# Moving the last addition of a softmax sum from VectorE to GpSimd, one weight-building unit behind the first output projection, and one weight load later

## The chip, the cores and the metric

The kernel runs on one NeuronCore of a Trainium2 chip. The metric is the device time of one execution in microseconds. The profile of one execution gives a span (first to last instruction) and, for every instruction, its start and its duration. Engines are written as in the profile: PE (TensorE), DVE (VectorE), ACT (ScalarE), POOL (GpSimd), SP (SyncE, which here only issues DMAs).

## The reference, cut to what matters

A graph of 512 nodes with 512 features goes through four residual layers: an attention layer with a feed-forward part, two GIN convolutions, a GCN layer and two relational (RGCN) layers. The change touches the attention and one weight of the relational layers.

```python
q, k, v = ((x @ W + b).reshape(N, H, HEAD) for W, b in ((Wq, bq), (Wk, bk), (Wv, bv)))
scores = jnp.einsum('nhd,mhd->nhm', q, k) / np.sqrt(HEAD)
scores = jnp.where(adj[:, None, :] == 0, -1000000000.0, scores)
attn = jax.nn.softmax(scores, axis=1)          # over the 8 heads, not over the nodes
attn_out = jnp.einsum('nhm,mhd->nhd', attn, v).reshape(N, D_OUT) @ Wo + bo
h1 = _layer_norm(x + attn_out, g1, be1)
...
w = jnp.einsum('rb,bio->rio', att, basis)      # relational weights from 30 bases
agg + x @ root + bias
```

## The kernel before

**The softmax over the heads.** The 512 x 512 scores of 8 heads are made in eight steps, `it` = 0 to 7. A step holds 128 nodes m on the partitions, 256 nodes n and the 8 heads, 128 x 2048 numbers. Since the softmax runs over the heads, its maximum and its sum are elementwise trees over the eight head slices: 4 + 4, 2 + 2, 1 + 1.

**One step, engine by engine.** PE writes the scores of step it+1 to the PSUM tensor `sbank` (`products`, L1490, and `exclude`, L1498, which masks missing edges), then the weighted sum of step it-1 (`attend`, L1513), then some units (below). ACT copies half of the scores (L616), DVE finds the maximum (`find_max`, L962 to L964) and subtracts it (`centre`, L1038, two instructions), ACT takes exp in place (L600). DVE then sums the heads in three additions: L1049 (128x1024 out), L1050 (128x512) and L1053 (128x256, into `row_sum`). ACT makes the reciprocal as exp(-ln) (`invert`, L608 and L610, each behind the loading of an activation table). Four heads are multiplied by it on DVE (L1065), four on POOL (`scale_heads`, L426); in the last step DVE multiplies all eight. The order of DVE's queue in one step is: L1049, L1050, L1053 of step it; L962, L963, L964 and the two of L1038 for step it+1; L1065 of step it; in steps 0 and 1 also the addition of a bias to a tile of v (L875).

**Where a product may start.** `products(it+1, pair)` overwrites the half of `sbank` that `centre(it)` has read. `attend(it)` waits for both multiplications of step it. `project(0)`, the first of four output projections (L1567), needs the first half of `centre(7)`, since it writes over that part of `sbank`.

**Units.** The relational weights are sums over 30 bases with 32 units per layer (64 in all). A unit is a DMA of 1 MB into a ring of four places (`bring`; L336 on SP's queue, issued when the unit four places earlier has been used) and eight matmuls of PE (L1357). They are put between other work by hand; `STEP_UNITS` is how many follow each attention step. Each fourth unit ACT copies the sums to `stage` and SP stores them.

**After the last step.** PE's order is `project(0)`, `attend(6)`, `project(1)`, `attend(7)`, one unit, `project(2)`, `project(3)`. `project(2)` waits for ACT's `take_ao(1)` (L621), which takes the result of `attend(7)` out of PSUM. On ACT's queue `take_ao(1)` stands behind `root(1, 0)` and `root(1, 1)`, the square roots (L466) of the norm of the first two projected tiles. DVE makes that norm tile by tile: L1082 (residual), L853 and L858 (statistics), L1073, L863, L1075; L1082 of tile 0 stands in DVE's queue behind L1065 of step 7.

**Weights.** POOL's queue issues the weight loads (`load_weight`, L398), each when the last reader of the place it overwrites is done (`LAST_READ`). `root1` is a weight of 1 MB for the first relational layer. It is loaded when `c2_1` is done ("c2_1_psum"). ACT and DVE split it into two parts after the GCN aggregation (`split_weight("root1")`, L490 and L1015). Between `c2_1` and that, PE has the transposes L1668 ("x4_psum"), units 55 to 59, and the aggregation over k (L1411) in the parts k = 0, unit 60, k = 1 to 3, unit 61; part k waits for `h_gcn_lo(k)` of DVE (L1208).

Of the kernel before, what the change touches and what calls it, by code (L numbers as in the profile page):

```python
# [25 lines left out]
ALU = mybir.AluOpType  # L26
# [5 lines left out]
C = D // P  # L32
# [52 lines left out]
def in_extra(n):  # L85

    return any(n in pair for pair in EXTRAS)


RING_UNITS = [n for n in range(2 * UNITS) if not in_extra(n)]  # L90
STEP_UNITS = (1, 2, 3, 3, 3, 3, 3, 0)
ATTENTION_BATCHES = (EARLY_UNITS + sum(STEP_UNITS)) // BATCH + 1
AGG0_BATCHES = 11

# [15 lines left out]
             "f2b": ("weight_parts", 2 * C), "c1_0": ("ff1_psum", C), "lin": ("ff1_psum", 2 * C),  # L110
             "c2_0": ("ff2_psum", C), "c1_1": ("ff2_psum", C),
             "c2_1": ("weight_parts", 7 * C), "gcn": ("weight_parts", 8 * C),
             "root1": ("c2_1_psum", C), "root2": ("c2_1_psum", C)}

AGG2_BANKS = H1T_BANKS = (0, 1, 4, 5)
T_ORDER = ("h1T", "ff1", "ff1_second", "hT2", "agg0", "agg1", "agg2")
# [12 lines left out]
def build(nc, x, src, dst, etype, weights, rows, cols, alphas, att, basis, scratch, out):  # L129
    with ExitStack() as ctx:  # L130
# [5 lines left out]
        def sem(name):  # L136
            if name not in names:
                names[name] = ctx.enter_context(nc.semaphore(name))
            return names[name]
# [5 lines left out]
        def places(*uses):  # L145

            made = []
            for use in uses[:-1]:
                with ExitStack() as early:
                    made += [early.enter_context(nc.sbuf_tensor(*t)) for t in use]  # L150
            return made + [ctx.enter_context(nc.sbuf_tensor(*t)) for t in uses[-1]]
# [10 lines left out]
        no_edge, row_sum, sum_tmp, adj, adjT_r = places(  # L162
            [("no_edge", [P, C, N], BF16), ("row_sum", [P, 2, N // 2], F32), ("sum_tmp", [P, 2, N // 2], F32)],
            [("adj", [P, C, N], F32)], [("adjT_r", [P, C, N], F32R)])
# [68 lines left out]
        four_sums = adjT[:, 0:2, :].rearrange("p c (a n) -> p (c a) n", a=2)  # L233
# [8 lines left out]
        def row(name):  # L242
            return rring[:, ROWS.index(name) % RSLOTS, :]
# [59 lines left out]
        def probs_of(it):  # L303
            return s01[:, (it % 2) * C:(it % 2 + 1) * C, :].rearrange("p c (a n) -> p (c a) n", a=2)
# [8 lines left out]
        def blk(t, c):  # L313
            return slice(c * t, (c + 1) * t)

        with nc.Block() as block:
# [54 lines left out]
            def _(pool):  # L371
# [22 lines left out]
                def load_weight(name):  # L394
                    i = WEIGHTS.index(name)
                    last, tiles = LAST_READ[name]
                    pool.wait_ge(sem(last), tiles)
                    pool.dma_start(weight(name), weights[i]).then_inc(sem(f"weight_{PLACE[name]}_loaded"), 16)  # L398

                def load_row(name, last):  # L400
                    i = ROWS.index(name)
                    pool.wait_ge(sem(last), C)
                    pool.dma_start(row(name), rows[i, :].partition_broadcast(P)).then_inc(
                        sem(f"row_slot{i % RSLOTS}_loaded"), 16)
# [18 lines left out]
                def scale_heads(it):  # L423
                    sc = probs_of(it)
                    pool.wait_ge(sem("row_inverse"), 2 * it + 2)
                    pool.tensor_tensor(sc[:, OWN_HEADS:, :], sc[:, OWN_HEADS:, :],  # L426
                                       row_sum[:, 1:2, :].to_broadcast([P, HEADS - OWN_HEADS, N // 2]),
                                       ALU.mult).then_inc(sem("pool_probs"), 1)

                scale_heads(0)  # L430
                scale_heads(1)
                load_row("g2", "v")
                for it in range(2, 2 * C - 1):
                    scale_heads(it)
                pool.wait_ge(sem("pv_used"), 2 * C)
                load_weight("f1b")
                pool.wait_ge(sem("o_psum"), C)
# [24 lines left out]
            def _(act):  # L462
# [133 lines left out]
                def exps(it):  # L596
                    for half in range(2):
                        act.wait_ge(sem("centred"), 2 * it + half + 1)
                        sc = probs_of(it)[:, 4 * half:4 * half + 4, :]
                        act.activation(sc, sc, ACT.Exp).then_inc(sem("exped"), 1)  # L600
# [25 lines left out]
                for it in range(2 * C):  # L626
# [5 lines left out]
                    if it + 1 < 2 * C:  # L632
                        exps(it + 1)
                    stage_units(STEP_UNITS[it])
                    if C - 1 <= it < 2 * C - 1:
# [180 lines left out]
            def _(dve):  # L816
                steps = [0]

                def step(ins):

                    steps[0] += 1
                    ins.then_inc(sem("dve_step"), 1)
                    return steps[0]

                def after(n):
                    dve.wait_ge(sem("dve_step"), n)
# [218 lines left out]
                for it in range(2 * C):  # L1045
                    sc = probs_of(it)
                    dve.wait_ge(sem("centred"), 2 * it + 2)
                    dve.wait_ge(sem("exped"), 2 * it + 2)
                    after(step(dve.tensor_tensor(four_sums, sc[:, 0:4, :], sc[:, 4:8, :], ALU.add)))  # L1049
                    after(step(dve.tensor_tensor(sum_tmp[:, :, :], four_sums[:, 0:2, :], four_sums[:, 2:4, :], ALU.add)))  # L1050
                    if it:
                        dve.wait_ge(sem("probs"), it)
                    dve.tensor_tensor(row_sum[:, 0, :], sum_tmp[:, 0, :], sum_tmp[:, 1, :], ALU.add).then_inc(  # L1053
                        sem("row_sum"), 1)
                    if it + 1 < 2 * C:
                        dve.wait_ge(sem("scores_psum"), 4 * it + 8)
                        dve.wait_ge(sem("scores"), it + 2)
                        find_max()
                        centre(it + 1)
                    if it == 2 * C - 1:  # L1060
                        split_weight("f1a")
                    dve.wait_ge(sem("row_inverse"), 2 * it + 2)
                    heads = OWN_HEADS if it < 2 * C - 1 else HEADS
                    own = sc[:, 0:heads, :]
                    dve.tensor_tensor(own, own, row_sum[:, 1:2, :].to_broadcast([P, heads, NH]),  # L1065
                                      ALU.mult).then_inc(sem("probs"), 1)
                    if it < 2:
                        take_v(2 + it)
# [259 lines left out]
            def _(pe):  # L1328
# [13 lines left out]
                def units(n):  # L1342


                    for u in (next(unit) for _ in range(n)):
                        b, g = divmod(u, BATCH)
                        if u == 0:
                            pe.wait_ge(sem("att_ready"), BATCH)
                        if g == 0 and b >= 2:
                            pe.wait_ge(sem("stage_ready"), b - 1)  # L1350
                        if g == 0 and b == EARLY_UNITS // BATCH:
                            pe.wait_ge(sem("v"), 1)
                        elif g == 0 and b == EARLY_UNITS // BATCH + 1:
                            pe.wait_ge(sem("v"), C)
                        wait_unit(pe, u)
                        for j in range(COLT):
                            mm = pe.matmul(unit_bank(b)[32 * j:32 * j + 32, :], attw[0:KB, u // UNITS, g, :],  # L1357
                                           unit_place(u)[0:KB, j, :], start=(g == 0), stop=(g == BATCH - 1),
                                           tile_position=(0, 32 * j), skip_group_check=True)
                        mm.then_inc(sem("basis_used"), 1)  # L1360
# [198 lines left out]
                def project(c):  # L1559

                    pe.wait_ge(sem("ao"), 2 if c < 2 else 4)
                    if c == 0:
                        need_weight(pe, "o")
                    if c < 2:
                        pe.wait_ge(sem("centred"), 4 * C - 1)
                    for k in range(C):
                        mm = pe.matmul(bank[C + c][:, :], qT[:, k, blk(P, c)], weight("o")[:, k, :], start=(k == 0),  # L1567
                                       stop=(k == C - 1))
                    mm.then_inc(sem("o_psum"), 1)

                pe.wait_ge(sem("no_edge"), C)
                for it in range(2 * C):
                    if it + 1 < 2 * C:
                        for pair in range(2):
                            products(it + 1, pair)
                            exclude(it + 1, pair, "scores_psum")
                    if it == 2 * C - 1:
                        project(0)
                    if it:
                        attend(it - 1)  # L1580
                    if it == 2 * C - 1:
                        project(1)
                    if it < 2:
                        qkv_tile(2 * C + 2 + it)
                    units(STEP_UNITS[it])
                attend(2 * C - 1)
                units(1)
                project(2)
# [218 lines left out]
```

## Time and profile before

| | |
|---|---|
| three runs | 455.17, 455.60, 456.53 us, median 455.6 |
| the profiled execution, its own time | 459.73 us |
| its span | 457.9 us, 1.8 us less than its own time |
| busy share of the span | PE 96%, DVE 76%, ACT 53%, POOL 9% |
| mean granted clock of TensorE | 0.993 |
| DMA | 99.22 MB, mean 217 GB/s |

The profiled execution is one execution, and it was longer than each of the three timed ones. The attention steps lie between 88 and 165 us of its span. Times in the rows are microseconds from the start of the span.

### The profile page before, as it was taken

What the parts mean: (1) busy time and instruction counts of PE and PEld (TensorE: products, weight loads), DVE (VectorE), ACT (ScalarE), POOL (GpSimd) and SP (SyncE); (2) the same over time, 40 slices, a digit from 0 to 9 for tenths busy, and PEclk for the clock granted to TensorE, in tenths of its full rate; (3) what the DMA queues carried; (4) which work ended last, traced back from release to release, by engine and by line L of the source; (5) the groups of instructions that cost most, each with busy time, mean ns of one, the idle gap of its engine ahead of it and who ended that gap; (6) DMA issues with size and microseconds to landing.
All of it is one profiled execution on the core that took longest, in us unless ns stands there. A gap on an engine that the chain in (4) does not pass through costs nothing.

```text
span 457.9 us, 6200 instructions
## 1 busy us (share of the span) xinstructions
PE 441.6 (96%) x2226; PEld 275.4 (60%) x2226; DVE 346.4 (76%) x736; ACT 243.6 (53%) x428; POOL 42.7 (9%) x59
## 2 busy tenths in 40 slices
PE   8999999899997999999999999999989999999997
PEld 3334453444432345768756867677357688888885
DVE  5999996899999849785879675766778695866212
ACT  5999994676897516562246335535662523511210
POOL 3240000024224002000010000010000000000000
PEclk9999999999999799999999999999999999999999
DMA  7997348426699747979089856687871740000002
GB/s 258 414 392 170 115 167 324 160 92 233 245 374 353 278 192 250 424 263 383 36 336 342 318 213 285 247 320 284 318 250 49 290 178 16 1 0 2 0 3 92
DMA packets 18090, 99.22 MB, mean 217 GB/s; under 512 B 2959, under 2 KB 3599, under 8 KB 7567
## 3 DMA queue, kind: packets, MB, share of 16 engines
q1 hardware_dynamic: 13191, 72.72, 42.4%
q0 software_dynamic: 4000, 25.18, 14.9%
q10 hardware_dynamic: 864, 0.86, 0.6%
q8 instruction: 22, 0.36, 0.3%
q14 instruction: 13, 0.11, 0.1%
HBM read 93.50 MB, written 5.25 MB: 216 GB/s over the span
## 4 chain that ended last, share of the span: by engine, by line
PE 72%; DVE 14%; DMA 10%; issue 2%; ACT 1%; DVEq 0%; SPq 0%
PE bank L1371 20%; PE sbank L1703 10%; DMA bring<-in_basis 7%; PE bank L1716 6%; PE sbank L1357 6%; PE sbank L1427 6%; PE sbank L1567 4%; PE bank L1688 4%; PE bank L1450 3%; PE bank L1357 3%; PE bank L1411 2%; DVE stat L853 2%; PE sbank L1411 2%; DMA wring<-in_weights 2%; PE bank L1513 2%; PE sbank L1490 2%
## 5 line engine op out<-in xcount | busy, mean ns | idle before, releaser
L1357 PE MATMUL sbank<-bring,attw 120*32 120x512 f32 x336 | 41.0, 599 | 2.2 <-DMA bring<-in_basis 2.2
L839 DVE TENSOR_SCALAR cnt<-iota_row,edge_f 128x512 bf16<-128x512 f16 x132 | 41.2, 347 | 0.4 <-PE sbank L1427 0.4
L466 ACT ACTIVATE stat<-stat,eps 128x1 f32<-128x1 f32 x32 | 9.4, 294 | 42.9 <-DVE stat L858 42.9
L1427 PE MATMUL sbank<-cnt,adjT 128*128 128x512 bf16 x132 | 30.6, 380 | 0.3
L576 ACT ACTIVATE adjT<-distance,edge_w,edge_f 128x128 bf16<-128x128 bf16 x61 | 29.3, 480 | 1.4 <-PE sbank L1427 1.4
L1281 DVE SCALAR_TENSOR_TENSOR y_lo<-sbank,gate,y_hi 128x512 fp32r<-128x512 f32 x16 | 11.8, 750 | 22.6 <-ACT y_hi L765 22.5
L497 ACT ACTIVATE s<-bank,colsb 128x512 f32<-128x512 f32 x24 | 16.4, 687 | 21.8 <-PE bank L1371 21.8
L1427 PEld LDWEIGHTS sbank<-cnt,adjT 128*128 128x128 bf16 x132 | 12.3, 98 | 21.7 <-DVE cnt L839 6.4
L1371 PE MATMUL bank<-hT_hi,w_hi 128*128 128x512 f32 x64 | 25.3, 395 | 0.0
L529 ACT ACTIVATE distance<-iota_row,edge_f 128x128 bf16<-128x128 f16 x61 | 24.3, 400 | 1.8 <-DVE edge_f L905 0.4
L1371 PE MATMUL bank<-hT_hi,w_lo 128*128 128x512 f32 x64 | 24.9, 390 | 0.0
L1371 PE MATMUL bank<-hT_lo,w_hi 128*128 128x512 f32 x64 | 24.9, 389 | 0.0
L1703 PE MATMUL sbank<-w_hi,xT_hi 128*128 128x512 f32 x64 | 24.9, 389 | 0.0
L1703 PE MATMUL sbank<-w_lo,xT_hi 128*128 128x512 f32 x64 | 24.9, 389 | 0.0
L1703 PE MATMUL sbank<-w_hi,xT_lo 128*128 128x512 f32 x64 | 24.9, 389 | 0.0
L836 DVE TENSOR_SCALAR adjT<-iota_row,edge_f,edge_w 128x128 bf16<-128x128 f16 x71 | 22.1, 312 | 2.0 <-PE sbank L1427 2.0
L765 ACT ACTIVATE y_hi<-sbank,gate 128x512 fp32r<-128x512 f32 x16 | 10.8, 688 | 23.8 <-PE sbank L1703 23.8
L1357 PE MATMUL bank<-bring,attw 120*32 120x512 f32 x144 | 19.0, 627 | 4.0 <-DMA bring<-in_basis 4.0
L600 ACT ACTIVATE s<-s 128x1024 f32<-128x1024 f32 x16 | 16.9, 1058 | 11.1 <-DVE s L1038 10.6
L426 POOL TENSOR_TENSOR s<-s,row_sum 128x1024 f32<-128x1024 f32 x7 | 16.6, 2374 | 59.1 <-ACT row_sum L610 59.1
L1357 PEld LDWEIGHTS sbank<-bring,attw 120*32 120x32 f32 x336 | 8.5, 109 | 22.0 <-issue 20.2
L1490 PE MATMUL sbank<-qkw 64*128 64x256 f32 x128 | 18.1, 402 | 2.1 <-DVE s L1038 2.0
(250 smaller groups left out, 1095.9 us busy)
## 6 DMA issues: line engine op xcount, KB each, us to landing
bring<-in_basis SPq DMA_DIRECT2D x59, 1024.0 KB, 9.7
wring<-in_weights POOLq DMA_DIRECT2D x8, 1024.0 KB, 10.0
landing<-in_weights POOLq DMA_DIRECT2D x4, 1024.0 KB, 5.1
w_scratch<-stage SPq DMA_DIRECT2D x16, 256.0 KB
hT<-in_weights POOLq DMA_DIRECT2D x4, 1024.0 KB, 8.4
qkw<-w_scratch POOLq DMA_DIRECT2D x2, 2048.0 KB, 8.0
rring<-in_rows POOLq DMA_DIRECT2D x12, 256.0 KB, 8.3
wring<-in_basis SPq DMA_DIRECT2D x2, 1024.0 KB, 12.9
```

The lines of the kernel that those rows point to most:

```text
L529: act.activation(distance[:, i % 2, :], iota[:, 0:P], ACT.Abs, scale=-1.0, bias=dst_lo[:, n:n + 1]).then_inc(sem("distance"), 1)
L576: act.activation(hot_d[:, n % HOT, :], distance[:, i % 2, :], ACT.Relu, scale=minus_w[:, n:n + 1], bias=weight_f[:, n:n + 1]).then_inc(sem ...
L836: dve.tensor_scalar(hot_d[:, n % HOT, :], iota[:, 0:P], dst_lo[:, n:n + 1], weight_f[:, n:n + 1], ALU.is_equal, ALU.mult).then_inc(sem("ho ...
L839: dve.tensor_scalar(hot_s[:, n % HOT, :], iota[:, :], src_f[:, n:n + 1], None, ALU.is_equal).then_inc(sem("hot_ready"), 1)
L1357: mm = pe.matmul(unit_bank(b)[32 * j:32 * j + 32, :], attw[0:KB, u // UNITS, g, :], unit_place(u)[0:KB, j, :], start=(g == 0), stop=(g == ...
L1371: mm = pe.matmul(bank[c][:, :], lhs[:, k, blk(P, c)], rhs[:, k, :], start=(k == 0 and i == j), stop=(k == C - 1 and i == 1))
L1411: mm = pe.matmul(bank[banks[c]][:, :], x[:, k, blk(P, c)].bitcast(dt), counts[:, k, :], start=(k == 0 and i == 0), stop=(k == C - 1 and i ...
L1427: pe.matmul(bank[7][:, :], hot_d[:, n % HOT, :], hot_s[:, n % HOT, :], start=(n == 0), stop=(n == ECH - 1)).then_inc(sem("hot_used"), 1)
L1490: pe.matmul(sbank[:, place_of(h), :], kT[at:at + HD, h // 2, blk(P, m)], qT[at:at + HD, h // 2, blk(NH, half_n)], start=(a == 0), stop=Fal ...
L1567: mm = pe.matmul(bank[C + c][:, :], qT[:, k, blk(P, c)], weight("o")[:, k, :], start=(k == 0), stop=(k == C - 1))
L1703: mm = pe.matmul(bank[C + c][:, :], (xT_hi, xT_lo)[i][:, k, blk(P, c)], (w_hi, w_lo)[j][:, rel * C + k, :], start=(k == 0 and i == j), sto ...
L1716: mm = pe.matmul(bank[c][:, :], counts[:, k, blk(P, c)], y[:, k, :].bitcast(dt), start=False, stop=(rel == RELS - 1 and k == C - 1 and i = ...
```

## The change

Of each step's three additions the last one goes from DVE to POOL: DVE signals `pair_sums` behind L1050, POOL adds the two halves into `row_sum`, and ACT waits for POOL's signal as it did for DVE's. POOL's queue then alternates: addition of step it, multiplication of step it (steps 0 to 6), and the addition of step 7. One unit goes from step 5 and is put behind `project(0)` in step 7; the number of units up to `attend(7)` stays 18. `root1` is loaded when the transposes L1668 are done, no longer when `c2_1` is.

```diff
-STEP_UNITS = (1, 2, 3, 3, 3, 3, 3, 0)
+STEP_UNITS = (1, 2, 3, 3, 3, 2, 3, 1)
...
-             "root1": ("c2_1_psum", C), "root2": ("c2_1_psum", C)}
+             "root1": ("x4_psum", C), "root2": ("c2_1_psum", C)}
...
-                scale_heads(0)
-                scale_heads(1)
-                load_row("g2", "v")
-                for it in range(2, 2 * C - 1):
+                def add_pairs(it):
+
+                    pool.wait_ge(sem("pair_sums"), it + 1)
+                    if it:
+                        pool.wait_ge(sem("row_inverse"), 2 * it)
+                    pool.tensor_tensor(row_sum[:, 0, :], sum_tmp[:, 0, :], sum_tmp[:, 1, :], ALU.add).then_inc(
+                        sem("row_sum"), 1)
+
+                for it in range(2 * C - 1):
+                    add_pairs(it)
                     scale_heads(it)
+                    if it == 1:
+                        load_row("g2", "v")
+                add_pairs(2 * C - 1)
...
-                    after(step(dve.tensor_tensor(sum_tmp[:, :, :], four_sums[:, 0:2, :], four_sums[:, 2:4, :], ALU.add)))
                     if it:
-                        dve.wait_ge(sem("probs"), it)
-                    dve.tensor_tensor(row_sum[:, 0, :], sum_tmp[:, 0, :], sum_tmp[:, 1, :], ALU.add).then_inc(
-                        sem("row_sum"), 1)
+                        dve.wait_ge(sem("row_sum"), it)
+                    dve.tensor_tensor(sum_tmp[:, :, :], four_sums[:, 0:2, :], four_sums[:, 2:4, :], ALU.add).then_inc(
+                        sem("pair_sums"), 1)
...
                     if it == 2 * C - 1:
                         project(0)
+                        units(STEP_UNITS[it])
                     if it:
                         attend(it - 1)
                     if it == 2 * C - 1:
                         project(1)
                     if it < 2:
                         qkv_tile(2 * C + 2 + it)
-                    units(STEP_UNITS[it])
+                    if it < 2 * C - 1:
+                        units(STEP_UNITS[it])
```

## Rows read from the trace of the kernel before

**Rows 1.** Stretches of the span: length, busy time of each engine, PEclk, DMA share, GB/s.

```profile
127.00:149.40 22.40, 17.97 (x140) 6.60 (x134) 21.95 (x24) 19.82 (x25) 7.11 (x3) 0.99 0.96 364
149.40:151.30 1.90, 1.90 (x9) 0.24 (x9) 1.86 (x3) 1.88 (x3) 0.00 (x0) 0.50 0.92 328
```

**Rows 2.** Timeline of PE, steps 5 to 7: start, duration, engine, line, idle before.

```profile
138.80 1.06 PE L1357 MATMUL bank<-bring,attw 120*32 120x512 f32 x8 [1.50 <-DMA bring<-in_basis]
...
146.98 1.06 PE L1357 MATMUL bank<-bring,attw 120*32 120x512 f32 x8 [1.03 <-DMA bring<-in_basis]
149.36 1.94 PE L1357 MATMUL bank<-bring,attw 120*32 120x512 f32 x8 [1.31 <-DMA bring<-in_basis]
151.22 5.97 PE L1567 MATMUL sbank<-wring,qkw 128*128 128x512 f32 x8
...
159.00 3.70 PE L1567 MATMUL sbank<-wring,qkw 128*128 128x512 f32 x8
...
165.75 7.13 PE L1567 MATMUL sbank<-wring,qkw 128*128 128x512 f32 x16 [0.18 <-ACT qkw L621]
```

**Rows 3.** Timeline of DVE: step 0, the end of step 2, and step 6 onward.

```profile
89.33 1.23 DVE L1049 TENSOR_TENSOR adjT<-s 128x1024 f32<-128x1024 f32 x1
...
91.31 0.43 DVE L1053 TENSOR_TENSOR row_sum<-sum_tmp 128x256 f32<-128x256 f32 x1
...
113.96 1.70 DVE L1065 TENSOR_TENSOR s<-s,row_sum 128x1024 f32<-128x1024 f32 x1
115.58 1.21 DVE L1049 TENSOR_TENSOR adjT<-s 128x1024 f32<-128x1024 f32 x1
...
145.65 2.36 DVE L1038 TENSOR_TENSOR s<-sbank,softmax_tmp 128x1024 f32<-128x1024 f32 x2
...
149.43 1.21 DVE L1049 TENSOR_TENSOR adjT<-s 128x1024 f32<-128x1024 f32 x1
...
154.15 2.28 DVE L1065 TENSOR_TENSOR s<-s,row_sum 128x2048 f32<-128x2048 f32 x1
157.43 0.69 DVE L1082 TENSOR_TENSOR vr<-sbank,hr 128x512 f32<-128x512 f32 x1 [0.99 <-PE sbank L1567]
...
159.96 0.75 DVE L1075 SCALAR_TENSOR_TENSOR vr<-vr,stat,rring 128x512 f32<-128x512 f32 x1
162.74 0.69 DVE L1082 TENSOR_TENSOR vr<-sbank,hr 128x512 f32<-128x512 f32 x1 [2.03 <-PE sbank L1567]
```

**Rows 4.** Groups of DVE by line, 86 to 160 us: count, busy us, mean ns.

```profile
L875 DVE TENSOR_TENSOR vr<-bank,rring 128x512 f32<-128x512 f32 x4 | 2.6, 680 | 0.0
```

**Rows 5.** Timeline of ACT, step 0: the reciprocal.

```profile
91.77 0.42 ACT L608 ACTIVATE row_sum<-row_sum 128x256 f32<-128x256 f32 x1 [0.35 <-DVE row_sum L1053]
...
93.50 0.42 ACT L610 ACTIVATE row_sum<-row_sum 128x256 f32<-128x256 f32 x1
```

**Rows 6.** Timeline of POOL: the multiplications of steps 0 and 2.

```profile
94.00 2.38 POOL L426 TENSOR_TENSOR s<-s,row_sum 128x1024 f32<-128x1024 f32 x1 [24.02 <-ACT row_sum L610]
...
112.20 2.37 POOL L426 TENSOR_TENSOR s<-s,row_sum 128x1024 f32<-128x1024 f32 x1 [4.38 <-ACT row_sum L610]
```

**Rows 7.** Groups of POOL by line, whole span: another computing instruction.

```profile
L388 POOL COPY attw<-attw 120x16 f32<-120x16 f32 x3 | 1.6, 557 | 14.6 <-DMA attw<-in_att 14.6
```

**Rows 8.** Timelines of POOL, PE and DVE around the load of `root1`.

```profile
321.06 0.53 POOL L398 DMA_DIRECT2D wring<-in_weights  x1 [18.93 <-PE bank L1371]
...
329.49 1.07 PE L1357 MATMUL sbank<-bring,attw 120*32 120x512 f32 x8 [0.90 <-DMA bring<-in_basis]
...
334.63 1.06 PE L1357 MATMUL sbank<-bring,attw 120*32 120x512 f32 x8 [1.29 <-DMA bring<-in_basis]
...
337.40 0.69 DVE L1208 TENSOR_TENSOR root_lo<-hr,root_hi 128x512 fp32r<-128x512 f32 x1 [1.54 <-ACT root_hi L738]
...
339.38 0.39 PE L1411 MATMUL bank<-adjT_r,root_hi 128*128 128x512 f32 x1
...
341.96 2.20 ACT L490 CAST root_hi<-wring 128x512 fp32r<-128x512 f32 x4
```

## The prediction

> **What bounds the kernel now.** I read the page's slices first (PE busy nearly everywhere, its clock low in one slice), then the chain that ended last, then the timelines of each engine between 88 and 166 us and the stretches cut out of them. The chain names DMA and PE for the end of the attention: from step 5 on PE stands before units whose data have not landed, 1.50, 1.03 and 1.31 us in the three longest waits, while the DMA engines are 96% busy [rows 1, 2]. Behind the last wait the granted clock is 0.50, the 1.2 GHz level; a unit takes 1.94 us in place of 1.06, `project(0)` 5.97 in place of the 3.70 of `project(1)` [rows 1, 2]. That half clock cost 0.88 + 2.27 = 3.15 us.
>
> The reader must see a second chain beside it. DVE has 21.95 us of work in the 22.40 us from 127 on [rows 1], and in most steps it doesn't run at its own speed. Its L1065 takes 1.70 us while POOL is still multiplying; POOL ends at 112.20 + 2.37 = 114.57, L1065 at 115.66, and the next step's L1049 starts at 115.58, 1.01 behind POOL's end [rows 3, 6]. The same 1.00 or 1.01 stands behind POOL's end in steps 4, 5 and 6. So a step of DVE is a loop of latency: sums, reciprocal on ACT, POOL's multiplication, 1.01 us, next step.
>
> How the two chains meet decides what a gain is worth. DVE's L1065 of step 7 ends at 154.15 + 2.28 = 156.43. Behind it stand the norm of tile 0, 159.96 + 0.75 - 157.43 = 3.28 (3.20 to the next start, which overlaps), and from tile 1's L1082 through `root(1, 1)` and `take_ao(1)` to `project(2)` 165.75 - 162.74 = 3.01 [rows 2, 3]. Starting 0.08 before L1065's end, as the next instruction does at 115.58, that is 156.43 - 0.08 + 3.20 + 3.01 = 162.56. PE alone would have been there at 165.75 - 0.18 = 165.57, or at 162.42 had its clock stayed up [rows 2]. In an execution with a full clock the DVE chain and the PE chain arrive together, and taking waits off PE alone buys nothing.
>
> Which kind are the timed executions? The profiled one took 459.73 us, the median of the runs is 455.6, which is 4.1 less, and 3.15 of these are the price of the half clock. I take the timed runs as mostly free of it, with a chance of 0.7. My sum is made for the profiled execution and then read against the median.
>
> **The change part by part.**
>
> *The unit.* Step 5 loses the unit that waited 1.50, and the last of step 6's becomes the one behind `project(0)`. The first half of `centre(7)` is over near 145.65 + 1.2 = 146.9 [rows 3], so `project(0)` can start about 147 in place of 151.22, and the DMA gets the 3.7 us of `project(0)` to bring the last unit. The load of the fourth unit after that of step 5 is issued later too, which leaves more of the busy DMA to the two before it. PE's own path gets 4 us shorter (7 with the clock). The cover for what is late next is gone with it: PE is early and waits for DVE.
>
> *The addition.* DVE loses eight L1053 of 0.43 [rows 3]. They would pay only if DVE's queue were the loop. What the loop sees is the way from L1050's end to ACT's logarithm: now 0.04 + 0.43 + 0.03, from 91.27 to 91.77 [rows 3, 5]. Then it is a handover to POOL, the addition, and a handover to ACT. Handover: ACT's end at 93.92 to POOL's start at 94.00 is 0.08 [rows 5, 6]; DVE to ACT is 0.04. The price of a 128x256 addition on POOL isn't in the trace. From below: a quarter of 2.37, 0.59 [rows 6]. From above: all of the 557 ns of the small copy as a fixed cost plus a quarter of the rest, 0.56 + 1.81 / 4 = 1.01 [rows 7]. The row nearest in kind is the multiplication, the copy has a strided pattern, so both ends are unlikely; I take the middle, 0.80. The way becomes 0.08 + 0.80 + 0.04 = 0.92, that is 0.42 more than 0.50.
>
> The Trainium skill, GPSIMD Engine Reference, section 3.1, gives 4497 ns for a float32 `tensor_tensor` addition of 2048 elements; with the row of 1024 elements a straight line gives an estimate of 0.78, and the sum below would be 0.2 us smaller by it. Its section 1 speaks against this change: POOL shares its SBUF interfaces with VectorE and contends with instructions that have two SBUF inputs. L1065 is one, and the 1.70 beside 1.21 for the same size without POOL agrees; L962 has a PSUM input and should not feel POOL's addition.
>
> Now the loop. In step 0 POOL's multiplication ends 96.38 - 89.33 = 7.05 behind L1049's start [rows 3, 6]; that becomes 7.47, and with 1.01 behind it a step takes 8.48. DVE's earlier `centre` can't help, since L1065 then only waits longer beside POOL. Steps 0 and 1 have a v tile besides, 0.60 each to the next start (0.68 with the overlap) [rows 4]. Seven steps: 7 x 8.48 + 1.20 = 60.56, so step 7 starts at 89.33 + 60.56 = 149.89, now 149.43 [rows 3]: 0.46 later. Step 7: L1049 and L1050 take 1.94, the way 0.92, the reciprocal from 91.77 to 93.92 takes 2.15 [rows 5], a handover 0.07: L1065 starts at 154.97 and ends at 157.25, 0.82 later than 156.43. `project(2)` then starts at 162.56 + 0.82 = 163.38. Against the profiled 165.75 that is 2.37 earlier, against an execution with a full clock 0.82 later. With 0.59 for the addition, each of eight ways is 0.21 shorter: 1.7 less; with 1.01, 1.7 more. POOL's remaining queue hides nothing of worth: the issue of `g2` stands behind the multiplication of step 1 and in front of the addition of step 2, and waits for a v tile that DVE makes before that step's sums, 2 us ahead.
>
> *The root weight.* Its load is now issued at 321.06, just when the ring's loads for units 59 and 60 are [rows 8]. Both units wait, 0.90 and 1.29. Issued when the transposes are done, some 4 us later (near 325), it leaves the first unit the bus alone; 1 MB at the 364 GB/s of a busy stretch [rows 1] is some 2.9 us. Of the 2.19 not all is gain: the aggregation's last part starts at 339.38, and needs the L1208 that ends at 337.40 + 0.69 = 338.09 and hangs on no unit [rows 8]. With 0.05 for the handover it can start at most 1.2 earlier; DVE's split of the next weight behind it holds nothing more. I take 1.1. The weight itself is read at 341.96 [rows 8], about 17 us after its new issue. Bounds: 0, if unit 60 is still late beside it, and 1.2.
>
> *Sum.* For an execution like the profiled one 459.73 - 2.37 - 1.1 = 456.3, with a full clock behind the change. Against the median: 455.6 + 0.82 - 1.1 = 455.3.
>
> **The rivals.**
>
> *The waits and the half clock are in the timed runs too (chance 0.24).* For it: the only execution with a trace has them. Against it: 4.1 us between it and the median. Then 455.6 - 2.37 - 1.1 = 452.1, faster.
>
> *The clock falls in a new gap (0.20), the case on the other side.* PE ends `attend(7)` near 159.2 (157.3, when L1065 is done, + 1.9) and the unit near 160.2, and then stands until 163.4: a gap of 3.2 us where a full-clock execution before has almost none. In the rows a gap of 1.50 left the clock up, gaps of 1.03 and 1.31 with one unit between brought it down [rows 1, 2]. If it falls, `project(2)` pays what `project(0)` paid, about 2.3: 455.3 + 2.3 = 457.6, slower. It decides once the gap is above some 2.3 us. The Trainium skill, TensorE: Matmul & The Clock Gate, Part 1, says that the array falls to half rate when it has been idle and regains the full one after sustained work; the trace agrees at 149.4. By that rule the longer gap makes this rival stronger than the one before it.
>
> *GpSimd's addition is dear (0.07)*: at 1.01 us and in every step on the loop, 455.3 + 1.7 = 457.0.
>
> *It is cheap (0.09)*: at 0.59, and the DVE chain gains: 455.3 - 1.7 = 453.6. A variant of it is that DVE's own queue is the loop after all and its 0.43 per step count.
>
> **How the numbers follow.** My case, the two parts nearly cancelling, has 0.40. I call 0.3% (1.4 us) what a measurement can tell from no change. My case is the same with 0.34, faster with 0.05, slower with 0.01; the first rival faster with 0.24; the clock rival slower with 0.20; the dear addition slower with 0.05 and the same with 0.02; the cheap one faster with 0.07 and the same with 0.02. That makes 0.36 faster, 0.38 the same, 0.26 slower. The range reaches to the first two rivals, 452.0 to 457.8. My case alone, by half of the spread of the addition and the bounds of `root1`: 454.3 to 456.6.
>
> **What would show it.** POOL has eight additions of about 0.8 us, each starting 0.08 behind L1050's end. L1049 starts 8.4 to 8.5 us apart, and L1065 takes 1.7 to 1.9 in every step, nowhere 1.21. No unit waits more than 0.5 us in step 6; `project(0)` starts at 147 and takes 3.7; PE's wait has moved to before `project(2)`, released by ACT's L621, at 163.4, and L1065 of step 7 ends near 157.3. Units 59 and 60 wait less than 0.5 us together. I am wrong if L1065 of step 7 ends before 156.4 (the loop isn't POOL's), if the clock is 0.50 anywhere behind 160, or if the runs gain 3 us, which would say that the timed executions before had the half clock.

## The result

The changed kernel takes 459.95 us in the median of four runs (459.44 to 460.67), the kernel before 456.06 in the median of four (455.17 to 456.70). The ratio is 1.0087, 95% interval 1.0067 to 1.0108: slower by 3.9 us, outside the range of the prediction and past its rival on the other side (457.6).

Every run lists its mean granted clock of TensorE, and that is the first thing to read here. In the four runs of the changed kernel it was 0.992 or 0.993. Of the kernel before, 34 runs beside the first experiments have a clock each (a 35th took 888 us and isn't counted): 22 of them 0.999 or 1.000, with a median of 456.12 us, 12 of them 0.949 to 0.996, with a median of 457.53. The profiled execution of before (0.993) was one of the rarer kind.

### The profile page after: what moved, and what is told of

Same layout as the page of the kernel before. It is cut to its first block, busy times and chain, and to the rows that moved or that the text cites. A ratio compares the mean times of both kernels' runs of the same rounds, so it can differ in the third digit from the quotient of the medians.

```text
span 458.2 us, 6207 instructions
## 1 busy us (share of the span) xinstructions
PE 441.5 (96%) x2226; PEld 276.9 (60%) x2226; DVE 346.7 (76%) x728; ACT 243.3 (53%) x428; POOL 49.4 (11%) x67
## 4 chain that ended last, share of the span: by engine, by line
PE 70%; DVE 18%; issue 4%; DMA 4%; ACT 2%; POOL 1%; DVEq 0%; SPq 0%; POOLq 0%
PE bank L1379 22%; PE sbank L1713 9%; PE sbank L1365 7%; PE bank L1726 6%; PE sbank L1435 6%; PE bank L1618 5%; PE bank L1698 4%; DVE s L1047 3%; DMA bring<-in_basis 3%; PE bank L1419 3%; PE sbank L1419 2%; PE bank L1458 2%; PE sbank L1345 2%; PE sbank L1575 2%; DVE softmax_tmp L971 2%
## 5 line engine op out<-in xcount | busy, mean ns | idle before, releaser
L1365 PE MATMUL sbank<-bring,attw 120*32 120x512 f32 x336 | 41.0, 599 | 3.1 <-DMA bring<-in_basis 3.1
L1365 PEld LDWEIGHTS sbank<-bring,attw 120*32 120x32 f32 x336 | 8.6, 109 | 22.6 <-issue 22.6
L1498 PE MATMUL sbank<-qkw 64*128 64x256 f32 x128 | 18.2, 402 | 3.2 <-DVE s L1047 3.0
L1047 DVE TENSOR_TENSOR s<-sbank,softmax_tmp 128x1024 f32<-128x1024 f32 x16 | 18.8, 1219 | 1.1 <-DVE softmax_tmp L973 0.8
L1498 PEld LDWEIGHTS sbank<-qkw 64*128 64x128 f32 x128 | 11.1, 186 | 13.8 <-DVE s L1047 7.4
```

The costliest lines, as they stand in the source:

```text
L1047: dve.tensor_tensor(sc[:, heads, :], sbank[:, heads, :], tmp[:, 0:1, :].to_broadcast([P, 4, NH]), ALU.subtract).then_inc(sem("centred"), 1)
L1498: pe.matmul(sbank[:, place_of(h), :], kT[at:at + HD, h // 2, blk(P, m)], qT[at:at + HD, h // 2, blk(NH, half_n)], start=(a == 0), stop=Fal ...
```

## The profile after

Timeline of PE in the changed kernel, steps 5 to 7 and behind (L1498 are the products, L1365 the units, L1575 the projections).

```profile
134.89 1.92 PE L1365 MATMUL bank<-bring,attw 120*32 120x512 f32 x16
138.19 1.13 PE L1498 MATMUL sbank<-qkw 64*128 64x256 f32 x8 [1.37 <-DVE s L1047]
...
146.37 1.07 PE L1365 MATMUL bank<-bring,attw 120*32 120x512 f32 x8 [1.17 <-DMA bring<-in_basis]
147.36 3.70 PE L1575 MATMUL sbank<-wring,qkw 128*128 128x512 f32 x8
151.00 1.06 PE L1365 MATMUL bank<-bring,attw 120*32 120x512 f32 x8
...
159.38 1.07 PE L1365 MATMUL bank<-bring,attw 120*32 120x512 f32 x8
163.10 8.83 PE L1575 MATMUL sbank<-wring,qkw 128*128 128x512 f32 x16 [2.65 <-ACT qkw L630]
```

It answers to [rows 2]. Three waits for DMA have become one (the wait of 1.37 is for VectorE), `project(0)` starts at 147.36 in place of 151.22 and runs at full clock. Then PE stands 2.65 us before `project(2)`, and the two projections behind it take 8.83 us where they took 7.13. The stretches show why (length, busy time of PE, PEld, DVE, ACT, POOL, clock, DMA share, GB/s):

```profile
160.00:162.00 2.00, 0.44 (x7) 0.00 (x0) 1.90 (x5) 0.21 (x2) 0.33 (x1) 1.00 0.51 160
162.00:164.00 2.00, 0.90 (x2) 0.49 (x3) 1.37 (x3) 1.04 (x3) 0.00 (x0) 0.98 0.99 418
164.00:166.00 2.00, 2.00 (x4) 0.78 (x3) 0.00 (x0) 0.00 (x0) 0.00 (x0) 0.50 1.03 434
166.00:168.00 2.00, 2.00 (x5) 0.85 (x4) 0.00 (x0) 0.00 (x0) 0.00 (x0) 0.67 0.32 135
```

The half clock has moved from before `project(0)` [rows 1] to behind the gap. DVE, to be read against [rows 3]:

```profile
89.50 1.22 DVE L1058 TENSOR_TENSOR adjT<-s 128x1024 f32<-128x1024 f32 x1
...
115.87 1.21 DVE L1058 TENSOR_TENSOR adjT<-s 128x1024 f32<-128x1024 f32 x1
...
122.44 1.88 DVE L1073 TENSOR_TENSOR s<-s,row_sum 128x1024 f32<-128x1024 f32 x1
124.24 1.21 DVE L1058 TENSOR_TENSOR adjT<-s 128x1024 f32<-128x1024 f32 x1
...
149.39 1.21 DVE L1058 TENSOR_TENSOR adjT<-s 128x1024 f32<-128x1024 f32 x1
150.63 0.69 DVE L1061 TENSOR_TENSOR sum_tmp<-adjT 128x512 f32<-128x512 f32 x1
151.24 3.02 DVE L1024 TENSOR_TENSOR w_lo<-landing,w_hi 128x512 fp32r<-128x512 f32 x4
154.72 2.29 DVE L1073 TENSOR_TENSOR s<-s,row_sum 128x2048 f32<-128x2048 f32 x1 [0.46 <-ACT row_sum L619]
```

POOL, to be read against [rows 6]:

```profile
117.89 0.73 POOL L435 TENSOR_TENSOR row_sum<-sum_tmp 128x256 f32<-128x256 f32 x1 [3.02 <-DVE sum_tmp L1061]
120.87 2.37 POOL L426 TENSOR_TENSOR s<-s,row_sum 128x1024 f32<-128x1024 f32 x1 [2.25 <-ACT row_sum L619]
...
151.40 1.11 POOL L435 TENSOR_TENSOR row_sum<-sum_tmp 128x256 f32<-128x256 f32 x1 [3.02 <-DVE sum_tmp L1061]
```

Steps without a v tile are 8.37 to 8.39 us apart (115.87 to 124.24, say). POOL's multiplication ends at 123.24, the next step starts 1.00 later: the loop through POOL, in every step now. Before, it was that in steps 2, 4, 5 and 6, and those without a v tile were 8.30 to 8.74 apart. The seven steps together did not get longer: 149.39 - 89.50 = 59.89 us, before 149.43 - 89.33 = 60.10. What got longer is step 7. L1073 of step 7 ends at 157.01, 7.62 behind that step's start; before it was 7.00. The instructions that follow on ACT show who holds PE:

```profile
161.79 0.29 ACT L475 ACTIVATE stat<-stat,eps 128x1 f32<-128x1 f32 x1 [2.90 <-DVE stat L867]
161.99 1.05 ACT L630 COPY qkw<-bank 128x512 f32<-128x512 f32 x2
```

`take_ao(1)` (L630) starts as soon as `root(1, 1)` in front of it has run, 2.5 us after `attend(7)` was done.

Around `root1`, against [rows 8], POOL and PE:

```profile
323.05 0.53 POOL L398 DMA_DIRECT2D wring<-in_weights  x1 [23.22 <-PE bank L1678]
...
326.14 1.04 PE L1365 MATMUL sbank<-bring,attw 120*32 120x512 f32 x8
...
333.28 1.06 PE L1365 MATMUL sbank<-bring,attw 120*32 120x512 f32 x8 [3.11 <-DMA bring<-in_basis]
...
335.05 0.63 PE L1419 MATMUL bank<-adjT_r,root_hi 128*128 128x512 f32 x1
...
341.56 1.07 PE L1365 MATMUL sbank<-bring,attw 120*32 120x512 f32 x8
```

A stretch behind unit 60:

```profile
335.00:337.00 2.00, 2.00 (x6) 1.56 (x5) 1.87 (x4) 0.58 (x2) 0.00 (x0) 0.50 0.93 209
```

Unit 59 waits no more, unit 60 waits 3.11, and behind it the aggregation's matmuls are 0.43 apart in place of 0.23, and last 0.63 in place of 0.39 [rows 8]: a second fall of the clock. From the last transposes to unit 61 PE takes 341.56 - 322.09 = 19.47 us; before it was 341.29 - 324.37 = 16.92.

## The experiments

All medians are of 12 runs unless said (four for the changed kernel); each kernel is compared with the kernel before on the same chip, whose medians there are 456.06 (four runs), 456.23, 456.33 and 456.28. In the last column stand the runs with a mean clock of at least 0.998 and their median. That mean is over the whole execution: it says that the clock fell, not where. Where it fell is known for the one profiled execution of each kernel alone. The intervals are some 1 us wide to either side, so differences of a few tenths between medians are not told apart from none.

| kernel | median us | ratio to before, 95% interval | clock kept |
|---|---|---|---|
| changed | 459.95 | 1.0087 (1.0067 to 1.0108) | 0 of 4 |
| root_only | 458.56 | 1.0044 (1.0021 to 1.0066) | 1 of 12, 456.61 |
| unit_only | 456.28 | 1.0004 (0.9983 to 1.0026) | 8 of 12, 456.14 |
| pool_only | 456.77 | 1.0004 (0.9983 to 1.0026) | 9 of 12, 456.72 |
| no_root | 458.25 | 1.0031 (1.0006 to 1.0055) | 3 of 12, 455.49 |
| after_warm | 457.31 | 1.0009 (0.9988 to 1.0030) | 12 of 12 |
| no_root_warm | 456.52 | 1.0003 (0.9987 to 1.0019) | 12 of 12 |
| after_swap | 455.78 | 0.9975 (0.9953 to 0.9997) | 3 of 12, 454.50 |
| swap_unit | 454.56 | 0.9962 (0.9944 to 0.9980) | 12 of 12 |
| root_later | 459.33 | 1.0058 (1.0038 to 1.0078) | 1 of 12, 457.89 |
| pool_swap (6 runs) | 453.69 | 0.9929 (0.9906 to 0.9952) | 6 of 6 |
| pool_swap_five | 454.39 | 0.9965 (0.9944 to 0.9986) | 6 of 12, 454.03 |
| swap_unit_five (8 runs) | 453.90 | 0.9949 (0.9930 to 0.9969) | 8 of 8 |

**Each part alone.** `root_only`:

```diff
-             "root1": ("c2_1_psum", C), "root2": ("c2_1_psum", C)}
+             "root1": ("x4_psum", C), "root2": ("c2_1_psum", C)}
```

> The kernel before with the later load of root1 alone. Theory (the profile after shows it): unit 60's data land 3.1 us late, the clock falls to 0.50 behind that wait, and the runs are 1.5 to 2.0 us slower than before. Rival (my prediction's term): the two waits of 0.9 and 1.3 go and nothing comes in their place, 1.1 us faster.

2.3 us slower than the median of before on the same chip (456.23), and the clock kept in 1 run of 12. Unit 60 waited 2.93 us in the profiled execution. The loss is there without the other two parts; my term of -1.1 had the wrong sign.

`unit_only`, the unit behind `project(0)` with the addition on VectorE:

```diff
-STEP_UNITS = (1, 2, 3, 3, 3, 3, 3, 0)
+STEP_UNITS = (1, 2, 3, 3, 3, 2, 3, 1)
...
                         project(0)
+                        units(STEP_UNITS[it])
...
```

> The kernel before with the unit moved behind the first projection alone. Theory: VectorE's chain sets the second pair of projections, so PE is early and stands some 2.5 us before project(2), the clock falls there, 1.5 to 2 us slower. Rival: the shorter PE path costs nothing or gains, 0 to 2 us faster, clock 1.00 behind 160.

Between the two: no difference over all runs, and none with the clock kept (456.14 beside 456.12). The gap was there, 1.75 us, and in the profiled execution the clock fell behind it:

```profile
154.11 3.70 PE L1567 MATMUL sbank<-wring,qkw 128*128 128x512 f32 x8
162.44 8.83 PE L1567 MATMUL sbank<-wring,qkw 128*128 128x512 f32 x16 [1.75 <-ACT qkw L621]
```

but it fell (there or elsewhere) in 4 runs of 12, no more often than before. PE's 4 us bought nothing: L1065 of step 7 ends at 156.36, before at 156.43, and `project(2)` hangs on what VectorE does behind it.

`pool_only`, GpSimd's addition with the units and `root1` as before:

```diff
-                    dve.tensor_tensor(row_sum[:, 0, :], sum_tmp[:, 0, :], sum_tmp[:, 1, :], ALU.add).then_inc(
-                        sem("row_sum"), 1)
...
+                    pool.tensor_tensor(row_sum[:, 0, :], sum_tmp[:, 0, :], sum_tmp[:, 1, :], ALU.add).then_inc(
+                        sem("row_sum"), 1)
```

> The kernel before with GpSimd's addition alone, units and root1 as before. Theory: VectorE's L1065 of step 7 ends some 0.5 us later, PE's DMA waits in steps 5 and 6 fill the time and no long gap stands before project(2): 0.3 to 0.8 us slower, no new clock fall. Rival: the addition carries the whole loss of 3.9 us.

With the clock kept 456.72 beside 456.12: 0.6 us slower, as expected in size, but the interval doesn't tell it from none. `project(2)` starts at 163.01 behind a gap of 1.38. This trace has nearly the pair of waits behind which the clock fell in the profiled execution of before, and here it did not fall:

```profile
146.18 1.07 PE L1365 MATMUL bank<-bring,attw 120*32 120x512 f32 x8 [1.24 <-DMA bring<-in_basis]
148.55 1.06 PE L1365 MATMUL bank<-bring,attw 120*32 120x512 f32 x8 [1.31 <-DMA bring<-in_basis]
```

`no_root`, the changed kernel with `root1` loaded as early as before:

```diff
-             "root1": ("x4_psum", C), "root2": ("c2_1_psum", C)}
+             "root1": ("c2_1_psum", C), "root2": ("c2_1_psum", C)}
```

> The changed kernel with root1 loaded as early as before. Theory: the attention part of the loss stays, 2.0 to 2.5 us over the kernel before, and 1.5 to 2 us less than the changed kernel; one clock fall (before 168) and none near 333. Rival: root1 was a gain and without it the kernel is 1 us slower than the changed one.

2.0 us over before and 1.7 under the changed kernel. The gap is 2.73 us, and the clock was kept in 3 runs of 12. Addition and unit, neither of them told from before alone, open together a longer gap than either does (2.73 beside 1.38 and 1.75): the unit makes PE early, the addition makes VectorE late.

**The clock by itself.** `after_warm` fills both gaps of the changed kernel with matmuls of zeros (`keep_clock(12)` is twelve of them); `no_root_warm` fills the first one of `no_root`. In the second gap they must wait until ACT has copied the sums out of the bank that they write, hence the `wait_ge`.

```diff
                 units(1)
+                keep_clock(12)
                 project(2)
...
                 aggregate("h_gcn_parts", "agg2_psum", order=ALL_BANKS[:C], banks=AGG2_BANKS)
+                pe.wait_ge(sem("stage_ready"), 2 * BATCHES - 2)
+                keep_clock(12, bank[7])
                 units(1)
```

> The changed kernel with twelve short matmuls of zeros (2.6 us) in each of PE's two gaps, before project(2) and before unit 60; results unchanged. Theory (the gaps cost twice, as a wait and as the half clock behind it): granted clock 1.000 in nearly all runs, 2.5 to 3.5 us faster than the changed kernel, that is 456.3 to 457.5. Rival (the waits themselves are the loss): at most 1 us faster than the changed kernel, 459 or more.

> The changed kernel with root1 early and twelve short matmuls of zeros in PE's gap before project(2). Theory: the attention part of the loss without its half clock, 0.3 to 0.9 us over the kernel before, clock 1.000 or 0.999 in nearly all runs. Rival: the clock isn't what the gap costs, 1.4 us or more over the kernel before as in no_root.

Both have the clock kept in 12 runs of 12. PE in `after_warm` starts `project(2)` at the same time as in the changed kernel (163.14 and 163.10) and goes on faster:

```profile
160.13 2.76 PE L1465 MATMUL sbank<-zeros 128*128 128x512 bf16 x12
...
163.14 7.13 PE L1575 MATMUL sbank<-wring,qkw 128*128 128x512 f32 x16 [0.24 <-ACT qkw L630]
```

So of the changed kernel's loss 459.95 - 457.31 = 2.6 us is the half clock; that it is most of the loss is shown by the ratios too, 1.0087 and 1.0009. What is left over before, 1.0 to 1.3 by the medians and by the interval not told from nothing, is waiting: 0.2 to 0.5 in the attention (`no_root_warm` over before; 0.6 by `pool_only`), 0.8 at unit 60 (457.31 - 456.52). The medians that are subtracted here come from different chips, so the split is no better than some tenths.

**The gate of the second pair of projections.** `after_swap` and `swap_unit` change one place of ACT's queue, in the changed kernel and in `unit_only`.

```diff
                 root(1, 0)
-                root(1, 1)
                 take_ao(1)
+                root(1, 1)
```

> The changed kernel with ACT's take_ao(1) ahead of root(1, 1). Theory (PE's gap before project(2) is the wait for tile 1's variance that stands ahead of take_ao(1) in ACT's queue): project(2) starts near 160.6 in place of 163.1, no clock fall there, 3.5 to 4.5 us faster than the changed kernel, 455.5 to 456.5. Rival (something else of the second half sets project(3) or the norm): less than 2 us faster.

> The kernel before with the unit moved and ACT's take_ao(1) ahead of root(1, 1), the addition still on VectorE and root1 early. Theory: the shorter PE path pays once the gate behind it is gone, project(2) starts near 160, 2 to 3 us faster than before, 453.2 to 454.2. Rival: VectorE's norm of tile 2 waits instead and gives it back, within 1 us of before.

In both `project(2)` starts behind a gap of 0.18, at 160.34 and 160.51. The changed kernel gets 4.2 us faster by it, which shows that this place in ACT's queue held PE. It still has the second fall, behind unit 60:

```profile
329.73 1.94 PE L1365 MATMUL sbank<-bring,attw 120*32 120x512 f32 x8 [3.12 <-DMA bring<-in_basis]
```

`swap_unit` beats before by 1.8 us (456.33 - 454.56; 1.4 beside the executions of before with the clock kept) and keeps the clock in all runs. The moved unit alone gave nothing, moved unit and swap together give this. No run has the swap without the moved unit, so how much of the 1.8 the swap would give by itself stays open.

**The weight later still.** `root_later` is the kernel before with the load behind unit 60.

```diff
-             "root1": ("c2_1_psum", C), "root2": ("c2_1_psum", C)}
+             "root1": ("basis_used", 61), "root2": ("c2_1_psum", C)}
```

> The kernel before with the load of root1 behind unit 60. Theory (what lands late at unit 60 is a matter of the bytes in flight with it, and the load behind the transposes shares with unit 60 where the early one shared with unit 59): neither unit waits over 1 us, 1 to 2 us faster than before unless the weight lands behind 341, where it would be the same. Rival (unit 60 is late through its own issue, not through root1): unit 60 waits 1 to 3 us all the same and the time is that of before or more.

Half of each. Without `root1` in flight unit 59 didn't wait and unit 60 waited 0.49; from the last transposes to unit 61 PE took 335.84 - 320.01 = 15.83 us, 1.1 less than before, which is the gain that I had ascribed to the changed kernel. But the weight took 13.2 us to land, and two engines stood:

```profile
329.99 0.53 POOL L398 DMA_DIRECT2D wring<-in_weights  x1 [32.21 <-PE sbank L1357]
...
343.24 2.19 ACT L490 CAST root_hi<-wring 128x512 fp32r<-128x512 f32 x4 [6.61 <-DMA wring<-in_weights]
```

DVE's half of that split stands in its queue before the sums of the GCN layer, and PE soon had to wait for what hangs on them. In the profiled execution the clock fell behind that wait, the only fall in it (a pair of units takes 3.57 in place of 1.92), and it was kept in 1 run of 12:

```profile
351.31 0.66 PE L1337 MATMUL sbank<-ident,hr 128*128 128x128 f32 x4 [3.24 <-ACT hr L781]
351.89 3.57 PE L1357 MATMUL sbank<-bring,attw 120*32 120x512 f32 x16
```

Against before 3.0 us were lost (459.33 beside 456.33). My clause "it would be the same" was too kind.

**Where the addition could pay.** `pool_swap` is `swap_unit` with GpSimd's addition. The two "five" kernels give VectorE five of the eight heads.

```diff
-OWN_HEADS = 4
+OWN_HEADS = 5
```

> The kernel before with the unit moved, take_ao(1) ahead of root(1, 1) and the addition on GpSimd, root1 early: against swap_unit it differs by GpSimd's addition alone. Theory (a step is a loop of latency through GpSimd, and the addition lengthens it): 0.4 to 0.8 us slower than swap_unit, L1065 of step 7 ends 0.5 to 0.6 later. Rival (VectorE's queue is the loop, the addition taken off it pays): 0.3 to 1 us faster than swap_unit.

> As pool_swap, with five heads multiplied on VectorE and three on GpSimd (four and four before); the results are those of the reference. Theory: GpSimd's multiplication takes 1.8 in place of 2.37, and VectorE's L1073 starts when it is nearly over; steps of about 8.1 in place of 8.4, 1 to 1.8 us faster than pool_swap, as far as PE follows. Rival (L1073 is slow of itself here, not through GpSimd): 0.3 us per step slower, 2 us in all.

> As swap_unit, with five heads on VectorE and three on GpSimd, the addition on VectorE. Theory: here VectorE's own queue becomes the loop, 0.3 more per L1065 against what the contention gave, within 1 us of swap_unit and slower than pool_swap_five; so the addition on GpSimd pays only with fewer heads there. Rival: the same gain as in pool_swap_five, the addition's place doesn't matter.

In `pool_swap` L1073 of step 7 ends at 154.53 + 2.29 = 156.82 and L1065 of `swap_unit` at 154.04 + 2.29 = 156.33, 0.5 earlier, the expected size. But it isn't the steps that are longer, as the expectation had it: step 7 starts 59.90 us behind step 0 in the one and 59.88 in the other. All of the difference comes in step 7 itself, 7.62 us to the end of the multiplication in place of 7.03:

```profile
149.20 1.21 DVE L1058 TENSOR_TENSOR adjT<-s 128x1024 f32<-128x1024 f32 x1
...
151.22 1.11 POOL L435 TENSOR_TENSOR row_sum<-sum_tmp 128x256 f32<-128x256 f32 x1 [3.02 <-DVE sum_tmp L1061]
```

And `project(2)` starts at 160.56 and 160.51, and the kernel isn't slower. Its ratio is lower, with intervals that overlap, and six runs on another chip don't settle that; that the addition costs anything once the gate is gone was not shown. `pool_swap_five` has steps of 8.09 to 8.22, L1073 being 1.48 to 1.73:

```profile
129.37 1.68 DVE L1073 TENSOR_TENSOR s<-s,row_sum 128x1280 f32<-128x1280 f32 x1
130.98 1.21 DVE L1058 TENSOR_TENSOR adjT<-s 128x1024 f32<-128x1024 f32 x1
```

L1073 of step 7 ends 1.9 earlier than in `pool_swap`. PE gets 0.8 of it (`project(2)` at 159.80), since it comes sooner to a unit that has not landed, and waits:

```profile
145.54 1.07 PE L1365 MATMUL bank<-bring,attw 120*32 120x512 f32 x8 [1.99 <-DMA bring<-in_basis]
```

and in half of the runs the clock wasn't kept. So the forecast gain of 1 to 1.8 us didn't come. `swap_unit_five` has steps of 8.42 with L1065 at 1.48 throughout, free of POOL, as expected; it was to be slower than `pool_swap_five`, and isn't told apart from the others in time. All three beat the kernel before; which is best these runs don't decide.

## Why the prediction was wrong

**The steps that held.** POOL's addition was put at 0.80 and takes 0.73, the handovers at 0.08 and 0.04 and are 0.08 to 0.09 and 0.03, a step at 8.48 and is 8.38. L1065 was to take 1.7 to 1.9 in every step up to 6 and takes 1.88 to 1.91. L1065 of step 7 was to end at 157.25 and ends at 157.01; `project(2)` to start at 163.38 and starts at 163.10. That a shorter PE path buys nothing while VectorE's chain stands (`unit_only`) and that the timed executions were mostly free of the half clock (22 of 34) held too. A unit in step 6 still waits 1.17, where I had said at most 0.5.

**Right by luck: the end of the loop.** The forecast of 157.25 has two errors that cancel. The seven steps were to grow from 60.10 to 60.56, and they take 59.89. Step 7 was to take 157.25 - 149.89 = 7.36 and takes 7.62, since POOL's addition lasts 1.11 there. It is the same in every trace with four heads on POOL: 59.89 to 59.92 for the seven steps in the seven kernels with the addition on POOL, 59.88 to 60.17 in the five without. The sum took step 0, where ACT waits for VectorE's sum, for all steps. In step 4 of before ACT comes to its logarithm 0.71 later than the sum is ready (126.28), held by its own queue. The addition on POOL fits into that:

```profile
125.86 0.42 DVE L1053 TENSOR_TENSOR row_sum<-sum_tmp 128x256 f32<-128x256 f32 x1
126.99 0.42 ACT L608 ACTIVATE row_sum<-row_sum 128x256 f32<-128x256 f32 x1
```

and in the changed kernel, whose step 4 starts 0.36 later:

```profile
127.02 0.42 ACT L617 ACTIVATE row_sum<-row_sum 128x256 f32<-128x256 f32 x1 [0.21 <-POOL row_sum L435]
```

An addition on POOL in steps 0 to 6 alone would have tested this; no run has it.

**The first step that failed: the choice between my case and the clock rival.** I had the gap (3.2 us; it is 2.65) and the price (2.3; the projections took 1.70 longer here), and counted the fall as a case of 0.20 beside a likeliest one with the clock kept. The runs have it the other way round: the kernel with a gap of 2.73 keeps the clock in 3 runs of 12 (`no_root`), the one with 1.75 in 8 (`unit_only`), the one with 1.38 in 9 (`pool_only`), the one without a gap in 12 (`swap_unit`), the kernel before in 22 of 34. The last of these and those of 1.75 and 1.38 are not told apart, and some of their falls may lie elsewhere, as the one of before does. My border of 2.3 us was none: in the profiled execution of `unit_only` the clock fell behind 1.75, in that of `pool_only` it stayed up behind 1.24 and 1.31 with a unit between. But the rows I held against each other, 1.50 without a fall and 1.03 + 1.31 with one, said that 2.7 lies on the far side, and I had called this rival the stronger one and still given it 0.20 against 0.24. The fall belonged into the likeliest case.

**The second: the term of -1.1 for `root1`.** Its sign was wrong. I gave the first unit the bus alone and let unit 60 follow, named "unit 60 is still late beside it" as a bound of 0, and didn't ask whether it could become later than before. It did: it landed 333.1 - 318.5 = 14.6 us after `c2_1`'s last tile, before 334.5 - 320.8 = 13.7. Behind the last transposes unit 60 started 11.2 us later in the changed kernel, 10.3 before, and 8.6 in `root_later`, where `root1` isn't in flight: in both orders unit 60 pays for the weight. Why it pays 0.9 more in the later one was not tested. It would fit that the early load was issued at 321.06, 0.8 us ahead of the ring's first (321.82), when the DMA moved nothing (0 GB/s from 320 to 322). With a wait of 3.11 in one piece the clock fell there too, for which I had no case at all. `root_later` shows that the 1.1 existed on PE's side; it belongs to a load behind unit 60, which lands too late.

**The sum.** Attention without its clock +0.2 to +0.6 (forecast +0.8), `root1` without its clock some +0.8 (forecast -1.1), the two falls +2.6 (forecast 0 in my case, +2.3 for one of them in a rival). Together 3.6 to 4.0; measured 3.9. The agreement is no proof: these are differences between the medians of before, `no_root_warm`, `after_warm` and the changed kernel, and add up to the whole by themselves.

The Trainium skill (GPSIMD Engine Reference, section 1) has the rule that POOL contends with VectorE instructions of two SBUF inputs. The traces agree: L1073 takes 1.88 to 1.91 beside POOL's multiplication and 1.21 without it, L1024 3.02 beside POOL's addition and 2.49 without it. L971, which has a PSUM input, keeps its 1.21 to 1.22 beside that addition.

## What to carry to other kernels

A wait that is harmless as a wait can cost twice on TensorE. When a change makes PE early, add up how long PE will stand before the next instruction that another engine holds back, and price the half clock behind it in the likeliest case and not in a rival once the gap is near those that brought it down before; filling the gap with dummy matmuls, or better removing what holds PE, is a cheap test. When a transfer is moved later, ask which transfer it will share the bus with instead, and whether the bus was idle where it used to run. And when an engine seems full, look for a distance that repeats: VectorE was busy without a gap, and still an operation of 0.42 us taken off its queue left the seven steps at 59.9 us. The multiplication behind it, which had run alone in steps 0, 1 and 3 (1.21), now ran into POOL's in every step (1.9).

## What the runs showed of the hardware that I had not expected

VectorE's multiplication beside POOL's ended 1.07 to 1.09 us behind POOL's end, whether it had begun 0.3 or 0.8 us ahead of that end: while both run, VectorE gets only 0.12 to 0.14 us of its 1.21 done. POOL's own took 2.36 to 2.39 us all the same. In step 7 of the changed kernel both got slower: POOL's addition took 1.11 in place of 0.73, and VectorE's four L1024 beside it 3.02, where the kernel before has 2.49 for the same four:

```profile
151.75 2.49 DVE L1015 TENSOR_TENSOR w_lo<-landing,w_hi 128x512 fp32r<-128x512 f32 x4
```

The price of a fallen clock isn't one number. Of the 94 counted runs of the kernel before that have a clock, 60 with 0.998 or more have a median of 456.04 us, 27 with 0.995 or 0.996 one of 457.38, and 7 with 0.993 or less one of 458.96: 1.3 or 2.9 us more. The traces show what differs. The granted clock was 0.50 from about 162.5 to 166.5 in `unit_only` (mean 0.996), and from about 162.3 to 169 in `no_root` (0.991), in both under `project(2)` and `project(3)`.
